# Two-part products of 448 columns in the projections of an attention and mixture-of-experts kernel

## What is computed

```python
xn = layernorm(x)
q, k_new, v_new = xn @ wq.T, xn @ wk.T, xn @ wv.T
k = concat([ctx, k_new]); v = concat([ctx, v_new])       # 375 + 112 rows each
x = x + softmax(q @ k.T / sqrt(512)) @ v @ wo.T
xn = layernorm(x)
top 2 of 8 experts by xn @ gate.T
x = x + sum over both: w_e * (silu(xn @ g_e.T) * (xn @ u_e.T)) @ d_e.T
```

## Time and profile before

| | |
|---|---|
| time, median of 3 runs | 457.0 us (456.34 to 458.38) |
| profiled execution, its own time | 458.06 us |
| its span, first to last instruction | 456.3 us |
| mean granted TensorE clock | 0.989 of 2.4 GHz |
| TensorE busy | 443.2 us, 97% of the span |
| VectorE, ScalarE, GpSimd busy | 343.9, 254.2, 99.1 us |
| four pairs | until about 160 us; the experts follow |

### The profile page before, as it was taken

One profiled execution on the slowest core, in us unless ns is written; L12 is line 12 of the kernel. 1 busy time (PEld: TensorE's weight loads), 2 busy tenths in 40 slices (PEclk: granted clock), 3 DMA queues, 4 the chain that ended last, 5 costly groups with the idle time before them and its releaser, 6 DMA issues.

```text
span 456.3 us, 7158 instructions
## 1 busy us (share of the span) xinstructions
PE 443.2 (97%) x2529; PEld 374.9 (82%) x2529; DVE 343.9 (75%) x645; ACT 254.2 (56%) x415; POOL 99.1 (22%) x128
## 2 busy tenths in 40 slices
PE   8999999999999999999999999999999999999991
PEld 6978888888888688888888888888888888888870
DVE  5867546466644659998988988988988988988850
ACT  4566434524533656666566566566666666666621
POOL 6061071344435443003003003003003003003002
PEclk9999999999999989999999999999999999999997
DMA  7996984424544365966766856856856856856203
GB/s 270 338 267 189 283 210 138 145 50 155 193 136 185 101 251 157 363 210 191 247 205 174 266 194 190 260 180 192 271 174 198 272 164 203 276 160 200 38 0 51
DMA packets 26911, 88.39 MB, mean 194 GB/s; under 512 B 2560, under 2 KB 8704, under 8 KB 26880
## 3 DMA queue, kind: packets, MB, share of 16 engines
q1 hardware_dynamic: 23296, 80.13, 53.8%
q0 software_dynamic: 3584, 7.88, 8.4%
HBM read 73.55 MB, written 14.45 MB: 193 GB/s over the span
## 4 chain that ended last, share of the span: by engine, by line
PE 92%; DVE 3%; ACT 2%; POOL 1%; DMA 1%; issue 0%; POOLq 0%; ACTq 0%
PE T L393 13%; PE PJ L393 13%; PE T L394 7%; PE PJ L394 6%; PE SC L472 3%; PE SC L473 3%; PE SC L474 3%; PE T L243 3%; PE PJ L230 3%; PE PJ L232 3%; PE PJ L231 3%; PE SC L260 3%; PE SC L264 3%; PE SC L262 3%; PE R L472 2%; PE R L473 2%
## 5 line engine op out<-in xcount | busy, mean ns | idle before, releaser
L842 DVE TENSOR_TENSOR ul<-ng,uh 128x1536 fp32r<-128x1536 f32 x64 | 112.5, 1758 | 2.4 <-ACT uh L609 1.5
L609 ACT ACTIVATE uh<-ng 128x1536 fp32r<-128x1536 f32 x64 | 94.7, 1480 | 0.0
L393 PE MATMUL T<-eb,uh 128*128 128x512 f32 x256 | 91.6, 397 | 0.0
L393 PE MATMUL PJ<-eb,uh 128*128 128x512 f32 x248 | 88.7, 397 | 0.0
L394 PE MATMUL T<-eb,ul 128*128 128x256 f32 x256 | 71.8, 281 | 0.0
L1295 POOL DMA_INDIRECT out<-ys,yidx x16 | 27.8, 1737 | 193.1 <-ACT ys L778 190.7
L394 PE MATMUL PJ<-eb,ul 128*128 128x256 f32 x248 | 69.6, 281 | 0.0
L393 PEld LDWEIGHTS T<-eb,uh 128*128 128x128 f32 x256 | 48.1, 188 | 11.5
L393 PEld LDWEIGHTS PJ<-eb,uh 128*128 128x128 f32 x248 | 46.6, 188 | 11.3
L394 PEld LDWEIGHTS T<-eb,ul 128*128 128x128 f32 x256 | 48.3, 189 | 1.4
L394 PEld LDWEIGHTS PJ<-eb,ul 128*128 128x128 f32 x248 | 46.7, 188 | 1.2
(11 more groups left out here) (228 smaller groups left out, 911.9 us busy)
## 6 DMA issues: line engine op xcount, KB each, us to landing
ng<-in_units SPq DMA_DIRECT2D x64, 768.0 KB, 4.7
vs<-in_ctxn SPq DMA_DIRECT2D x8, 768.0 KB, 5.2
kTs<-in_ctxT SPq DMA_DIRECT2D x8, 750.0 KB, 5.7
slots<-zero SPq DMA_DIRECT2D x8, 514.0 KB, 12.4
xe<-slots SPq DMA_DIRECT2D x8, 514.0 KB, 7.1
wTs<-in_weights SPq DMA_DIRECT2D x8, 512.0 KB, 8.2
out<-x_all SPq DMA_DIRECT2D x8, 224.0 KB
x_all<-in_x SPq DMA_DIRECT2D x1, 896.0 KB, 20.4
```

The lines of the kernel that those rows point to most:

```text
L393: nc.tensor.matmul(o[:, :].rearrange("p (h s) -> p h s", h=2), wh, both[:, k, :, :], start=k == 0, stop=False)
L609: nc.scalar.activation(o, i, ACT.Copy).then_inc(s, 1)
L842: v.tensor_tensor(o, whole, hi.bitcast(F32), ALU.subtract).then_inc(s, 1)
```

## The change

The first three chunks of pairs 1 to 3 are made in another way (nine chunks); chunk 3 of these pairs and all of pair 0 stay. `xTh` and `xTl` become the two halves of one buffer `xb`, so that both are one moving operand of 448 columns. Per block of features there is one product of `wTh` with both halves and one of `wTl` with the high half. The high-by-low part then lies in the columns 224 to 447 of the bank and has to be added: ScalarE copies these columns to `pt` (`half_pj`), VectorE adds them to the other 224 and writes `qf` (`sum_pj`), and the old split goes on from `qf`. One output block now fills one bank, so that a chunk takes both `SC[0]` and `SC[1]`, and the waits of chunks 1, 2 and 3 are on `pj_sum`.

```diff
+        pt = sb("pt", [128, 2, 2 * S], F32)
+        qf = sb("qf", [128, 2, 2 * S], F32)
-        xTh = sb("xTh", [128, KT, 2 * S], F32R)
-        xTl = sb("xTl", [128, KT, 2 * S], F32R)
+        xb = sb("xb", [128, KT, 2, 2 * S], F32R)
+        xTh, xTl = xb[:, :, 0, :], xb[:, :, 1, :]
...
+        def pe_proj_wide(c):
+            w = c // 2
+            for h in range(2):
+                bank = SC[h]
+                m = 2 * (c % 2) + h
+                ms = slice(128 * m, 128 * m + 128)
+                for k in range(KT):
+                    nc.tensor.matmul(bank[:, 0:4 * S].rearrange("p (u t) -> p u t", u=2), wTh[w][:, k, ms], xb[:, k, :, :],
+                                     start=k == 0, stop=False)
+                    last = nc.tensor.matmul(bank[:, 0:2 * S], wTl[w][:, k, ms], xTh[:, k, :], start=False, stop=k == KT - 1)
+            last.then_inc(pj, 1)
...
-                pe_proj(0, SC[0])
+                pe_proj_wide(0)
...
-                pe.wait_ge(expd, B + 1)
-                pe_proj(1, SC[1])
+                pe.wait_ge(pj_sum, 6 * p + 2)
+                pe_proj_wide(1)
...
-                pe.wait_ge(pj_lo, 4 * p + 5)
-                pe_proj(2, SC[0])
+                pe.wait_ge(pj_sum, 6 * p + 4)
+                pe_proj_wide(2)
                 pe_wo(pe, B, 1, PJ[1])
                 pe_x2T(pe, A, 0, T[0])
-                pe.wait_ge(pj_lo, 4 * p + 6)
+                pe.wait_ge(pj_sum, 6 * p + 6)
                 pe_proj(3, SC[1])
...
+            def half_pj(p, c):
+                act.wait_ge(pj, 4 * p + c + 1)
+                for h in range(2):
+                    copy(pt[:, h, :], SC[h][:, 2 * S:4 * S], pj_copy)
...
                 if more:
+                    half_pj(p + 1, 0)
                     hi_c(A + 2, 0)
                     hi_pj(p + 1, 0, SC[0])
...
+            def sum_pj(p, c):
+                n = 2 * (3 * p - 3 + c)
+                dve.wait_ge(pj_lo, 4 * p + c)
+                for h in range(2):
+                    dve.wait_ge(pj_copy, n + h + 1)
+                    v.tensor_tensor(qf[:, h, :], SC[h][:, 0:2 * S], pt[:, h, :], ALU.add).then_inc(pj_sum, 1)
...
                 if more:
                     x2_norms(A, 0)
+                    sum_pj(p + 1, 2)
                     lo_pj(p + 1, 2, SC[0])
                 x2_stats(B, 1, PJ[1])
```

More of the change, by code:

```diff
@@ L206, in build_kernel @@
         pj, pj_hi, pj_lo = sem("pj"), sem("pj_hi"), sem("pj_lo")
+        pj_copy, pj_sum = sem("pj_copy"), sem("pj_sum")
         c_hi, c_lo = sem("c_hi"), sem("c_lo")
@@ L626, in hi_x @@
                 copy(xTh[:, :, a * S:a * S + S], bank[:, 0:KT * S].rearrange("p (k t) -> p k t", k=KT), x_hi)
+            def half_pj(p, c):
+                act.wait_ge(pj, 4 * p + c + 1)
+                for h in range(2):
+                    copy(pt[:, h, :], SC[h][:, 2 * S:4 * S], pj_copy)
             def hi_pj(p, c, bank):
-                act.wait_ge(pj, 4 * p + c + 1)
-                v = bank[:, 0:4 * S].rearrange("p (m t) -> p m t", m=2)
+                if p and c < 3:
+                    act.wait_ge(pj_sum, 2 * (3 * p - 3 + c) + 2)
+                    v = qf[:, :, :]
+                else:
+                    act.wait_ge(pj, 4 * p + c + 1)
+                    v = bank[:, 0:4 * S].rearrange("p (m t) -> p m t", m=2)
                 m = 2 * (c % 2)
@@ L743, in body @@
                     hi_o(A, 0, T[1])
+                    half_pj(p + 1, 1)
                     hi_c(A + 3, 1)
@@ L747, in body @@
                 if more:
+                    half_pj(p + 1, 2)
                     hi_v(A + 2, 0)
@@ L882, in lo_x @@
                    xTh[:, :, a * S:a * S + S], x_lo)
+            def sum_pj(p, c):
[4 more added lines that the diff above has]
+                    v.tensor_tensor(qf[:, h, :], SC[h][:, 0:2 * S], pt[:, h, :], ALU.add).then_inc(pj_sum, 1)
             def lo_pj(p, c, bank):
                 dve.wait_ge(pj_hi, 4 * p + c + 1)
-                w = bank[:, 0:4 * S].rearrange("p (m t) -> p m t", m=2)
+                w = qf[:, :, :] if p and c < 3 else bank[:, 0:4 * S].rearrange("p (m t) -> p m t", m=2)
                 m = 2 * (c % 2)
@@ L1064, in body @@
                 if more:
+                    sum_pj(p + 1, 0)
                     lo_c(A + 2, 0)
@@ L1078, in body @@
                 if more:
+                    sum_pj(p + 1, 1)
                     lo_c(A + 3, 1)
```

## The result

| | before | changed |
|---|---|---|
| time, median of 5 runs | 457.09 us (456.34 to 458.38) | 464.36 us (463.82 to 464.82) |
| profiled execution | 458.06 us | 464.36 us |
| its span | 456.3 us | 462.6 us |
| mean granted TensorE clock | 0.989 | 0.985 |

The account below looks back on a forecast made before the run. TensorE was taken as the bound, busy for 443.2 of 456.3 us. The terms -1.2 + 5.7 + 0.2 + 0.5 + 0.8 = +6.0 us, against a median of 457.0, gave 463.0 us; 8 in 10 within 459.9 to 464.7.

Parts of the forecast that it names:

- The saving on TensorE: In the nine wide chunks, one 448-column product replaces two of 224, at 72 places: -1.2 us.
- ScalarE's copies push the context keys: Pair 1, chunk 0: the keys' rounding queues behind the new copies, moving `idx` by +1.66 us, with no TensorE wait.
- The wait in pair 1: Chunk 3 waits for chunk 2's additions, queued on VectorE behind `x2_norms(A, 0)`, which waits for the scatters: +5.7 us.
- The failed step: Pair 1: the first scatter's extra delay belongs to the program's first indirect DMA, so the scatters move 1.66 us with `idx`.
- the scatters don't move: Rival for pair 1: the first scatter's delay runs from GpSimd's idle start; wait 4.1 us, total 461.1 us, chance 0.25.
- Not slower: the delay isn't met again: Rival for pair 1: first scatter follows `idx` by 0.8 us, chunk 3 0.8 late; 457.3 us, chance 0.08.
- Pair 0: Context keys go 2.05 us later, delaying `oTl`, for which TensorE then waits: +0.5 us (0.3 to 0.7).
- Pair 2: Later scatters delay L931 and the sums, so chunk 3 starts slightly late: +0.2 us (0 to 0.4).
- The clock: TensorE's clock falls to half level around the pair 1 wait, partly within it: +0.8 us (0 to 1.8).

Follow-up runs that it names:

- the wait alone: Kernel before, with chunk 3 waiting for the low part of chunk 2 instead of chunk 1, behind `x2_norms(A, 0)`: 465.69 us, ratio 1.0171.
- both orders: Changed kernel with chunk 2's additions ahead of `x2_norms(A, 0)` and context keys ahead of copies and additions of chunks 0 and 1: 457.94 us, ratio 0.9999.

## Why the prediction was right, and where it was not

**The saving on TensorE** (forecast -1.2 us, 16 products in 2.53 us): right. A wide chunk took 2.52 us, and pairs 1 and 2 came out 0.44 and 0.46 us shorter by it, so about 1.4 us for nine chunks. The Trainium skill ("TensorE: Matmul & The Clock Gate", section "Back-to-back issue gap") has a formula with about 2.5 ns for each product, by which it would be 0.2 us; but the skill gives it for a product by itself and says that in a stream the weight loads count as well. The trace of this stream does not follow the formula: it has about 0.21 us from a 448-column product to the next and 0.10 to 0.11 from one of 224.

**ScalarE's copies push the context keys** (+1.66 us, on to `idx`): right. The keys went from 75.89 to 77.75 and `idx` from 80.26 to 82.14, of which 0.26 is the later start of chunk 0 (74.22 to 74.48). ScalarE's timeline in the changed kernel:

```profile
77.26 0.60 ACT L628 ACTIVATE pt<-SC 128x224 f32<-128x224 f32 x2 [1.02 <-PE SC L283]
77.75 1.46 ACT L628 ACTIVATE kTh<-kTs 128x1500 fp32r<-128x1500 f32 x1
```

**The wait in pair 1** (+5.7 us): the mechanism and the place were right, 5.34 us was measured, and the runs show it from both sides: the wait alone brings the loss to the old products, and an earlier scatter or moved norms take it from the wide ones. **The failed step** is how the forecast got from 4.1 to 5.7: "This extra belongs to the first indirect DMA of the program", and all would move by 1.66. The first scatter did not move by even 0.01 us, the added indirect DMA in pair 0 had no such extra, and neither had the first scatters behind GpSimd's additions, which were the first indirect DMAs of their programs. What made L970 run 1.50 us later were two terms that the forecast had held fixed: that same scatter took 2.04 us and not 1.21, which put the second one from 87.53 to 88.36, and from there to L970 it was 7.67 us and not 7.00. The second of these need not be the change's: the kernel before with the wait alone has 7.64 us, and the kernels in which VectorE waits for this landing have 6.6 to 8.2. So the sum was nearly right for a wrong reason, by luck. The scatter did follow `idx` in part, not in its start but in its length. Among the eight kernels with the late start, it took 1.21 us in the three where `idx` was written 3.6 us after GpSimd fell idle, 1.29 and 1.51 us in the two where it was 5.0 us, and 1.91 to 2.05 us in the three where it was 5.3 us. The rival "the scatters don't move" had the start right and the time wrong (461.1).

**Not slower: the delay isn't met again** (chance 0.08, 457.3 us): this did not happen by itself, but the run with two tiny additions makes exactly this case, and it gives 456.69 us and a wait of 0.68 where the rival had 0.8. One figure in that rival was wrong by its own sum: the sign turns where the scatter follows `idx` by about 0.5 us (the rival's 0.8 us gives +0.3), not by 1.1.

**Pair 0** (+0.5 us): right. TensorE waited for `oTl` in the output projection of A,

```profile
46.21 0.46 PE L235 MATMUL PJ<-wTh,oTh 128*112 128x512 f32 x1 [0.34 <-DVE oTl L873]
```

and the pair, which should have been some 0.45 us shorter, was 0.10 us longer, so 0.55. **Pair 2** (+0.2 us): no wait. (The forecast has the landing at 128.4 and yet L931 at 128.2; its own 0.2 us needs 128.4.) The transposes of x2 and chunk 3 follow each other,

```profile
135.77 0.55 PE L248 MATMUL T<-ident,x_all 112*128 112x112 f32 x4
136.08 0.68 PE L265 MATMUL SC<-xb,wTh 128*128 128x224 f32 x4
```

since L970 waited there 0.70 us for GpSimd's `rs` and not for a scatter. TensorE's delay from pair 1 is not what saved it: with the two small additions TensorE has hardly any, and pair 2 has no wait there either.

**The clock** (+0.8 us, 0 to 1.8): right in kind, and this is the term that was mis-sized: 1.66 us, shown by the run that keeps TensorE busy. The forecast let a good part of the low clock fall into the wait. In the trace nearly none did: the window from 94 to 97 us, all of it idle, still shows 1.00,

```profile
94.00:97.00 3.00, 0.00 (x0) 0.00 (x0) 0.97 (x3) 0.00 (x0) 0.00 (x0) 1.00 0.12 9
```

and the low level began with the work. The Trainium skill ("TensorE: Matmul & The Clock Gate", section "Why this matters for your kernels") warns that a long wait for a DMA between products makes them run at half rate; the trace agrees, with 0.86 us for four products and later 0.45.

The sum of the forecast against its own basis was +6.0 us, and the profiled executions differ by 6.3: -1.4 and not -1.2, 5.3 and not 5.7, 0 and not 0.2, 0.55 and not 0.5, 1.66 and not 0.8, and 0.15 from ahead of the change. So the good sum owes something to errors that cancel. Against the medians it is 7.3 us. The profiled execution of the kernel before was 1 us above its median, while that of the changed kernel lay on it, so the 1.06 us that the forecast took off was not there to take; with the 0.3 us of the sum, that is the 1.4 us by which 463.0 came out short. Both profiled executions had the low clock at the start of the experts.

**Why the first scatter is late at all** the runs leave half open. The table has its start in every kernel, against the write of `idx` that it needs, GpSimd's idle time ahead of it, and the start of an 8 KB transfer of instructions by DMA (queue `q14 instruction` in the profile; times in us):

| kernel | after `idx` | GpSimd idle | after the transfer |
|---|---|---|---|
| before | 5.6 | 9.23 | 2.07 |
| changed | 3.7 | 8.97 | 2.06 |
| the wait alone | 5.6 | 9.23 | 2.07 |
| TensorE busy in the wait | 3.7 | 8.96 | 2.07 |
| additions ahead of the norms | 3.8 | 9.10 | 2.07 |
| both orders | 4.1 | 9.04 | 2.07 |
| norms moved, wide and old products | 4.3, 5.8 | 9.26, 9.47 | 2.07, 2.06 |
| an indirect DMA in pair 0 | 1.3 | 6.59 | transfer comes later, at 84.86 |
| 512-column additions, on before | 1.1 | 3.99 | transfer at 62.41 |
| 8-column additions, on before | 1.1 | 4.41 | transfer at 62.22 |
| 8-column additions, on changed | 1.1 | 6.01 | transfer at 62.90 |

In the eight kernels whose GpSimd program is that of before, it starts 9.0 to 9.5 us after GpSimd's last work, whatever `idx` does. In the four with any instruction added ahead of it, it starts 1.1 to 1.3 us after `idx`. The last column points at the arrival of its code. In all eight late kernels a transfer of instructions begins between 83.1 and 84.5 us, in the kernel before at 83.95:

```profile
q14 instruction: 1, 0.01, 19.3%
```

(the queue's line for the window 83.90 to 84.00 us), and the scatter follows its start by 2.06 to 2.07 us each time, whatever `idx` and the idle time do. With additions ahead of the scatter a transfer comes at 62.2 to 62.9 us and none in these places; with the indirect DMA in pair 0 it comes after the scatter has started. The profile doesn't say whose instructions a transfer brings, and no run moved the transfer by itself, so this is the likely cause and not a proven one. Why it comes so late is open: in all eight kernels it begins in the last 0.5 us of the load of the context's values (768 KB, 81.25 to 84.18 us before the change).

One other suspect is out: the first scatter also waits for zeros that SyncE writes into `slots` (`zeroed`), but these were issued at 42.1 to 47.4 us and all had landed 18.1 us later at most.

## What to carry to other kernels

A new wait on an engine's queue inherits everything ahead of it there: before making TensorE wait for a helper's instruction, look at what that one stands behind, and above all at an idle note that is free today. A reordering may only shift such a stall to the next consumer; moving the waiting instruction behind all that TensorE needs, or making the transfer start on time, removes it. And price a wait of several microseconds on TensorE with a low clock behind it as well: here 1.7 to 2.4 us on top of 4 to 5. Before medians that lie 1 or 2 us apart are compared, look in the traces for a stretch whose clock differs from one execution to the next.

## What the runs showed of the hardware

- An indirect DMA on GpSimd started 3.7 to 5.8 us after the write of its indices, and 9.0 to 9.5 us after the engine fell idle, in eight kernels. Two 8-column additions ahead of it, 0.35 us of work, took the 3.7 to 5.8 us down to 1.1.
- In all eight it started 2.06 to 2.07 us after an 8 KB transfer of instructions began. In the four kernels without the delay, no such transfer came between 78 us and the scatter's start.
- The recorded length of that scatter was 1.21 us where `idx` came early in GpSimd's idle time (3.6 us in) and 1.91 to 2.05 us where it came later (5.3 us in). Some of the late start may therefore pass for work of the instruction.
- In the wait of 5.12 us, TensorE's clock was still granted in full from 94 to 97 us (1.00), and it was mostly at the low level from 97 to 100 us (0.56), when TensorE worked again. In the wait of 3.98 us it was at the low level already from 94 to 97 us, in which the wait ended (0.50), and stayed there to 100 us. Products that nobody read, in the same place, kept it at 1.00.
- A wait of 1.74 us left the clock at 1.00. Waits of 0.51 and 1.06 us, with 0.6 us of work between them, were followed by 0.59 from 102 to 105 us in one kernel, and waits of 0.29 and 1.06 us by 1.00 in another.
- The same 16 transposes took 2.03 us in four profiled executions and 2.85 to 3.63 us at a lower granted clock in eight.
